# Attention of layer 0: value products of two groups in one PSUM tile, with one copy, turn and division per pair

## The reference, cut to what matters

```python
qvk = (h @ Wqvk).reshape(b, s, 3, H, HD)
q, v, k = (qvk[:, :, 0], qvk[:, :, 1], qvk[:, :, 2])
scores = jnp.einsum('bshi,bthi->bsth', q, k)
...
scores = scores + mask[None, :, :, None]
scores = scores / math.sqrt(d)
weights = jax.nn.softmax(scores, axis=2)
wv = jnp.einsum('bsth,bthi->bshi', weights, v).reshape(b, s, d)
return wv @ Wo
```

## Time and profile before

| what | value |
|---|---|
| median of 3 runs | 783.85 us (783.3 to 787.15) |
| span of the profiled execution | 765.3 us |
| median of the runs less that span | 18.55 us |
| PE busy | 703.9 us, 92% |
| PEld (weight loads) busy | 526.3 us, 69% |
| DVE busy | 546.6 us, 71% |
| ACT busy | 419.5 us, 55% |
| POOL busy | 327.7 us, 43% |
| mean granted TensorE clock | 0.994 of full speed |

### The profile page before, as it was taken

How to read it: one execution, slowest core, us unless ns; L and a number is a source line. 1 busy time by engine, 2 the same in 40 slices (tenths; PEclk the granted TensorE clock), 3 DMA queues, 4 the chain that set the end, 5 groups by cost and what they waited for, 6 DMA issues and landing times.

```text
span 765.3 us, 17690 instructions
## 1 busy us (share of the span) xinstructions
PE 703.9 (92%) x6133; PEld 526.3 (69%) x6133; DVE 546.6 (71%) x1053; ACT 419.5 (55%) x802; POOL 327.7 (43%) x433
## 2 busy tenths in 40 slices
PE   5787788998899978989898999999999999999997
PEld 4643445556755547757666888888888888888885
DVE  6878997885678866779886766666665666666665
ACT  5645665676477678677664444444444444444442
POOL 3765643783758860147694631212122221222222
PEclk9999999999999999999999999999999999999999
DMA  6984655431134420012114611112121212111100
GB/s 188 261 239 137 179 133 201 167 95 49 51 120 129 142 85 1 12 33 61 54 43 117 156 52 56 56 41 69 41 69 41 69 41 59 50 52 58 41 15 14
DMA packets 63795, 66.51 MB, mean 87 GB/s; under 512 B 6512, under 2 KB 41840, under 8 KB 63728
## 3 DMA queue, kind: packets, MB, share of 16 engines
q1 hardware_dynamic: 62128, 63.23, 27.7%
q0 software_dynamic: 1024, 2.12, 1.0%
q10 hardware_dynamic: 576, 0.27, 0.1%
HBM read 47.46 MB, written 17.99 MB: 86 GB/s over the span
## 4 chain that ended last, share of the span: by engine, by line
PE 75%; DVE 9%; issue 5%; ACT 4%; DMA 3%; POOL 2%; SPq 1%; ACTq 0%; POOLq 0%; DVEq 0%
PE ps L1763 25%; PE ps L1992 22%; PE ps L1876 3%; DVE m L1241 3%; PE ps L1683 3%; PE ps L1587 3%; PE ps L1796 2%; PE ps L1831 2%; PE ps L1593 2%; PE ps L1597 2%; PE ps L1897 1%; DMA qk_parts<-qk_p 1%; PE ps L1601 1%; PE ps L1688 1%; PE ps L1580 1%
## 5 line engine op out<-in xcount | busy, mean ns | idle before, releaser
L963 ACT ACTIVATE f_h<-ps 128x512 fp32r<-128x512 f32 x256 | 153.3, 599 | 197.6 <-PE ps L1763 197.6
L1463 DVE SCALAR_TENSOR_TENSOR f_l<-ps,f_h 128x512 fp32r<-128x512 f32 x256 | 175.9, 691 | 112.5 <-ACT f_h L963 111.3
L1763 PE MATMUL ps<-x_hl,w_h 128*128 (+1 forms) x512 | 200.3, 391 | 0.0
L783 POOL TENSOR_TENSOR acc<-acc,yt 128x512 f32<-128x512 f32 x55 | 70.9, 1289 | 249.8 <-DVE yt L1501 249.8
L877 ACT ACTIVATE probs<-ps 128x1536 f32<-128x1536 f32 x64 | 92.8, 1450 | 34.4 <-PE ps L1606 33.8
L1763 PEld LDWEIGHTS ps<-x_hl,w_h 128*128 128x128 f32 x512 | 96.1, 188 | 19.6
L682 POOL TENSOR_SCALAR_AFFINE_SELECT probs<-probs 128x512 f32<-128x512 f32 x128 | 78.4, 637 | 59.8 <-ACT probs L877 59.5
L1992 PE MATMUL ps<-f_l,w_h 128*128 128x512 f32 x256 | 99.8, 390 | 1.3 <-DVE f_l L1463 1.3
L1992 PE MATMUL ps<-f_h,w_h 128*128 128x512 f32 x256 | 99.7, 390 | 0.0
L1763 PE MATMUL ps<-x_hl,w_l 128*128 (+1 forms) x256 | 99.6, 389 | 0.0
L1992 PE MATMUL ps<-f_h,w_l 128*128 128x512 f32 x256 | 99.6, 389 | 0.0
(11 more groups left out here) (225 smaller groups left out, 1328.2 us busy)
## 6 DMA issues: line engine op xcount, KB each, us to landing
gate_b<-gate_rows SPq DMA_DIRECT2D x64, 256.0 KB, 3.3
qk_parts<-qk_p SPq DMA_DIRECT2D x16, 512.0 KB, 3.8
k_st<-qk_parts SPq DMA_DIRECT2D x64, 96.0 KB
q_st<-qk_parts SPq DMA_DIRECT2D x64, 96.0 KB
y_tok<-zero SPq DMA_DIRECT2D x8, 512.0 KB, 2.9
w_raw<-in_w_e SPq DMA_DIRECT2D x16, 256.0 KB, 2.7
x_rows<-xn_rows SPq DMA_DIRECT2D x8, 260.0 KB, 3.2
w_up<-in_w_up SPq DMA_DIRECT2D x8, 256.0 KB, 2.7
```

Of the source, the lines that this page charges most:

```text
L783: nc.gpsimd.tensor_tensor(acc[:, :], acc[:, :], yt[:, e % 2, :], ALU.add).then_inc(summed, 1)
L963: nc.scalar.activation(r32(f_h[:, m % 4, :]), ps[:, m % 4, :], ACT.Relu).then_inc(f_hi, 1)
L1463: nc.vector.scalar_tensor_tensor(out=r32(f_l[:, m % 4, :]), in0=ps[:, m % 4, :], scalar=0.0, in1=f_h[:, m % 4, :], op0=ALU.max, op1=ALU.su ...
L1763: last = nc.tensor.matmul(dst, r32(lhs[i]), r32(rhs[j]), start=(k == 0), stop=(k == 2))
```

## The change

- `v_ring` has 48 columns per pair of heads in place of 16 per head: values of the first head, ones, zeros, then values of the second and ones. An even group multiplies with columns 0 to 31 and starts the accumulation; the odd group multiplies with columns 16 to 47 and ends it. Each product gives 32 rows.
- The copy from PSUM (`evacuate_pair`), the turning (`turn_out`) and the division (`divide_pair`) happen once per pair: copy in even slots, turning and division in odd slots. The turning stands ahead of `mask_late`, and so does the search for the experts' slots (slot 21).
- Both tiles of turned heads are made in one slot.
- `ps_m` lies in bank 0, in the bank of the early scores. So `mask_early` of the next group waits for `mneg_done` instead of `early_max`, and it stands inside `scores`, behind L1597 and the first two of the four L1601. `weigh` no longer waits for `mneg_done`.
- At the start, the maxima of group 1 are turned before the scores of group 2.
- The host permutes the weights of queries and keys so that pairs of heads fit (`by_depth`).

```diff
-        v_ring = sb("v_ring", [P, 2, TB, H0, 2 * HD0], where=era)
+        v_ring = sb("v_ring", [P, 2, TB, H0 // 2, 6 * HD0], where=era)
...
-            return 4 * b + 8 + (t if b < B - 2 else 0)
+            return 4 * b + 8
...
-        ps_m = ps[0:2 * GH, 6, S:S + P]
+        ps_m = ps[0:2 * GH, 0, 0:P]
...
-            nc.gpsimd.memset(v_ring[:, :, :, :, :], 1.0).then_inc(zeroed, 1)
+            nc.gpsimd.memset(v_ring[:, :, :, :, :], 0.0).then_inc(zeroed, 1)
             pool.wait_ge(zeroed, 6)
+            nc.gpsimd.memset(v_ring.rearrange("p u t i c -> p (u t i) c")[:, :, HD0:5 * HD0 + 1:4 * HD0], 1.0).then_inc(zeroed, 1)
+            pool.wait_ge(zeroed, 7)
...
-            def evacuate(g):
-                act.wait_ge(pv_done, num(g) + 1)
-                if past(g, 2):
-                    act.wait_ge(o_turned, num(g) - 1)
-                nc.scalar.activation(o_ring[:, at(g, 2), :], ps_o, ACT.Copy).then_inc(o_evac, 1)
+            def evacuate_pair(i):
+                act.wait_ge(pv_done, 2 * i + 2)
+                if i >= 2:
+                    act.wait_ge(o_turned, i - 1)
+                nc.scalar.activation(o_ring[:, i % 2, :], ps_o, ACT.Copy).then_inc(o_evac, 1)
...
-                if past(g, 3) and within(plus(g, -3), G0):
-                    evacuate(plus(g, -3))
+                if num(g) % 2 == 0 and 4 <= num(g) <= G0 + 2:
+                    evacuate_pair(num(g) // 2 - 2)
...
                     act.wait_ge(rstd_ready, B + 2)
+                    act.wait_ge(pv_done, G0 - 1)
...
-                if n >= 4 and within(plus(g, -4), G0):
-                    divide(plus(g, -4))
+                if n % 2 == 1 and 5 <= n <= G0 + 3:
+                    divide_pair((n - 5) // 2)
...
+                nc.vector.reciprocal(rden[:, i % 2, :, :], heads[:, :, :, HD0]).then_inc(inverted, 1)
+                dve.wait_ge(inverted, i + 1)
+                nc.vector.tensor_tensor(wv_tok[:, b % 2, :, half * D // 2:(half + 1) * D // 2].rearrange("p t (h d) -> p t h d", h=2 * GH),
+                                        heads[:, :, :, 0:HD0], rden[:, i % 2, :, :].unsqueeze(3).broadcast_to([P, TB, 2 * GH, HD0]), ALU.mult).then_inc(wv_put, 1)
...
                 if past(g, 2):
-                    pe.wait_ge(early_max, before_it(g))
+                    pe.wait_ge(mneg_done, num(g))
...
                 pe.wait_ge(mrow_in[at(g, 4)], div(g, 4) * 16 + 16)
+                for u in range(2):
+                    turned_first(g, u, 0)
+                if both:
+                    mask_early(far)
                 for n in range(2):
...
-                for n in range(2):
-                    for u in range(2):
-                        turned_first(g, u, n)
+                for u in range(2):
+                    turned_first(g, u, 1)
...
-                if past(g, 1):
-                    pe.wait_ge(o_evac, num(g))
-                pe.wait_ge(mneg_done, min(n + 3, G0))
-                if n >= 8 and n % GPB0 < TB:
-                    pe.wait_ge(wvn_done, (n - 8) // GPB0 * TB + (n % GPB0 + 1 if n < G0 else TB))
+                if num(g) % 2 == 0 and num(g) >= 2:
+                    pe.wait_ge(o_evac, num(g) // 2)
+                if n >= 8 and n % GPB0 == 0:
+                    pe.wait_ge(wvn_done, (n - 8) // GPB0 * TB + TB)
+                rows = slice(k % 2 * 2 * HD0, k % 2 * 2 * HD0 + 4 * HD0)
                 for h in range(GH):
-                    nc.tensor.matmul(ps_o[32 * h:32 * h + 2 * HD0, :], v_ring[:, u, 0, k * GH + h, :],
+                    nc.tensor.matmul(ps_o[32 * h:32 * h + 4 * HD0, :], v_ring[:, u, 0, k // 2 * GH + h, rows],
...
-                                     start=True, stop=False, skip_group_check=True)
+                                     start=(k % 2 == 0), stop=False, skip_group_check=True)
...
+                if n == 2:
+                    turn_max((0, 1))
+                    keep_on(7, 2)
                 scores_alone((0, n))
-                if n:
+                if n == 1:
                     keep_on(7, 2)
-                    turn_max((0, n - 1))
+                    turn_max((0, 0))
                     keep_on(7, 2)
...
+                if n == FIND:
+                    pe.wait_ge(wv_put, (FIND - 5) // 2)
+                    find_slots()
+                if n % 2 == 1 and 5 <= n <= G0 + 3:
+                    turn_out((n - 5) // 2)
                 if within(plus(g, 3), G0):
                     mask_late(plus(g, 3))
...
-                if past(g, 4) and within(plus(g, -4), G0):
-                    turn_out(plus(g, -4))
                 if within(plus(g, 2), G0):
                     turn_max(plus(g, 2))
-                if within(plus(g, 3), G0):
-                    mask_early(plus(g, 3))
...
-            def turn_out(g):
-                pe.wait_ge(o_evac, num(g) + 1)
-                if past(g, 1):
-                    pe.wait_ge(wv_put, num(g))
-                if g[1] % GPB0 == 3 and past(g, 7):
-                    pe.wait_ge(x_attn, div(plus(g, -7), GPB0) + 1)
+            def turn_out(i):
+                pe.wait_ge(o_evac, i + 1)
+                if i >= 1:
+                    pe.wait_ge(wv_put, i)
+                if i % 2 == 1 and i >= 3:
+                    pe.wait_ge(x_attn, (i - 3) // 2 + 1)
```

More of the change, by code:

```diff
@@ L155, in build @@
         wvn = sb("wvn", [P, 2, S], where=era)
-        rden = sb("rden", [P, 2, TB, GH], where=era)
-        v_ring = sb("v_ring", [P, 2, TB, H0, 2 * HD0], where=era)
+        rden = sb("rden", [P, 2, TB, 2 * GH], where=era)
+        v_ring = sb("v_ring", [P, 2, TB, H0 // 2, 6 * HD0], where=era)
         m8 = sb("m8", [P, 2, GH, TB], where=era)
@@ L855, in put_heads0 @@
             def put_heads0(b, t):
-                act.wait_ge(wv_mm, 2 * b + t + 1 if b < B - 2 else 2 * b + 2)
+                act.wait_ge(wv_mm, 2 * b + 2)
                 if b >= 2:
                     act.wait_ge(wo_mm, b - 1)
-                nc.scalar.activation(wvn[:, b % 2, t * P:(t + 1) * P], ps_heads(t if b >= B - 2 else 0), ACT.Copy).then_inc(wvn_done, 1)
+                nc.scalar.activation(wvn[:, b % 2, t * P:(t + 1) * P], ps_heads(t), ACT.Copy).then_inc(wvn_done, 1)
             for n in range(2):
@@ L866, in slot @@
                     negate_max(plus(g, 2))
-                if past(g, 3) and within(plus(g, -3), G0):
-                    evacuate(plus(g, -3))
+                if num(g) % 2 == 0 and 4 <= num(g) <= G0 + 2:
+                    evacuate_pair(num(g) // 2 - 2)
                 for b in range(B):
-                    for t in range(TB):
-                        if heads_turned(b, t) == num(g):
+                    if heads_turned(b) == num(g):
+                        for t in range(TB):
                             put_heads0(b, t)
@@ L1317, in low_x, with divide_pair @@
                 nc.vector.tensor_tensor(r32(x_hl[:, 1, ds(b * S, S)]), ps_t1(v % 2), x_hl[:, 0, ds(b * S, S)], ALU.subtract).then_inc(xl_put, 1)
[L1319 to L1329, removed]
+            def divide_pair(i):
+                b, half = divmod(i, 2)
+                dve.wait_ge(o_turned, i + 1)
+                if half == 0 and b >= 2:
+                    dve.wait_ge(wv_mm, 2 * b - 2)
+                heads = ps_tok.rearrange("p (t h r) -> p t h r", t=TB, h=2 * GH)
+                nc.vector.reciprocal(rden[:, i % 2, :, :], heads[:, :, :, HD0]).then_inc(inverted, 1)
+                dve.wait_ge(inverted, i + 1)
+                nc.vector.tensor_tensor(wv_tok[:, b % 2, :, half * D // 2:(half + 1) * D // 2].rearrange("p t (h d) -> p t h d", h=2 * GH),
+                                        heads[:, :, :, 0:HD0], rden[:, i % 2, :, :].unsqueeze(3).broadcast_to([P, TB, 2 * GH, HD0]), ALU.mult).then_inc(wv_put, 1)
             def add_attention(b):
@@ L1724, in slot @@
                         attention_out(b)
-                    for t in range(TB):
-                        if heads_turned(b, t) == n:
-                            turn_heads(b, t)
+                    if heads_turned(b) == n:
+                        turn_heads(b)
                 if n == COUNT:
                     pe.wait_ge(counted, 3)
-                if n == FIND:
-                    pe.wait_ge(wv_put, FIND - 4)
-                    find_slots()
-                if past(g, 4) and within(plus(g, -4), G0):
-                    turn_out(plus(g, -4))
                 if within(plus(g, 2), G0):
                     turn_max(plus(g, 2))
-                if within(plus(g, 3), G0):
-                    mask_early(plus(g, 3))
                 if within(g, G0):
```

29 lines of the change are left out of this document (15 added, 14 removed).

## The result

The changed kernel takes 789.3 us (median of 9 runs, 787.32 to 792.29) against 786.2 for the kernel before on the same chip (9 runs): ratio 1.006, 95% interval 1.0046 to 1.0075. It is slower by 0.6%; the forecast was 781.6, range 775.0 to 786.5. A second comparison, with the set of runs 1 to 4, gives the same, 1.0064 (1.0039 to 1.0088).

The account below looks back on a forecast made before the run. DVE's loop (2.77 us) bound most slots, PE's path (3.03) those with attention output, DVE's routing work eleven slots. Terms 1.0 - 0.4 - 4.3 + 2.6 - 1.1 = -2.2 took 783.85 to 781.6 us, range 775 to 786.5.

Parts of the forecast that it names:

- start-up: First slots: group 1's maxima must leave the bank before group 2's scores, 1.7 late, 0.7 given back: +1.0, bounds 0.5 and 1.7.
- slots 0 to 8 and 20 to 23: Forecast for slots 3 to 8 and 21 to 23: routing work on DVE, divisions gone from even slots; estimate -0.4 us.
- 8 to 20: DVE-bound routing stage, eleven slots: 34.0 against 38.35 us, -4.3.
- steady, 37 slots: 15 slots before the experts and 22 after go from 2.85 to 2.92 us on PE's path: +2.6.
- end: Last groups: one round of copy, turn and division leaves the final chain: -1.1 us, bounds 0 and -2.5.
- all under PE's 2.86 and 3.09, which take over: Routing stage: plain DVE slots of 2.8, 2.3 and 2.7 us fall below PE's path, which then sets them.
- ACT's loop with a late negation, 2.75: On ACT, when negated maxima come behind the exponential, the loop becomes 2.75 us, below PE's.
- The idle 0.55 before the division goes too: Routing stage on DVE: the 0.55 us wait for turned outputs vanishes, since they are turned half a slot earlier.
- The two crossings more, 0.20 a slot: On PE, the moved mask adds two changes between all-row and half-row matmuls, 0.10 us each: +0.20.
- The second rival: Mask's wait for negated maxima becomes the bound; at 0.2 latency 0.13 late in 53 slots, +6.9, 788.5 us; chance 0.15.
- the prediction's own sign (above 0.05 a slot): The forecast would be wrong if PE's wait for the negated maxima were above 0.05 us a slot.
- 18.5 us lie outside the span: Profiled execution spans 765.3 us, median 783.85; the 18.5 more was put around the span and left alone.

Follow-up runs that it names:

- runs 1 to 4: Kernel before again, 784.35 us; changed kernel again, 789.69; kernel before with only moved maxima and mask, 789.9; with only pairing, sums lost, 777.27.
- runs 1, 2: The kernel before, unchanged, for a second profile: 784.35 us; the changed kernel, unchanged, for a second profile: 789.69 us.
- run 3: Kernel before with only the maxima moved to the early scores' bank, the early mask moved and the changed start order: 789.9 us, ratio 1.008.
- run 1: The kernel before, unchanged, for a second profile: 784.35 us, ratio 0.9998, span 779.1.
- Run 7: Changed kernel with one more 32-column matmul over 48 rows in each of the 64 slots: ratio 1.0079 to the kernel before.
- Run 8: Changed kernel with ACT's four token-mark scalings moved from behind the exponential to ahead of the next one: ratio 1.0062 to the kernel before.
- runs 6, 7: Changed kernel with one more 32-column matmul per slot, over 128 rows: ratio 1.0169 to before; over 48 rows: 1.0079.
- run 5: Kernel before with pairing alone, sums kept by plain fp32 matmuls without start flag for odd maxima and second heads' turn: 768.16 us, ratio 0.9962.
- run 9: Kernel before with pairing alone, sums kept by turns without start flag for odd maxima and second heads' turn: 774.24 us, ratio 0.9874.

## Why the prediction was wrong

In the order of its own sum:

| term | forecast | measured | from |
|---|---|---|---|
| start-up | +1.0 | +1.3 | POOL's L619/L621 to the first exponential, 4.12 and 5.45 |
| slots 0 to 8 and 20 to 23 (forecast: 3 to 8, 21 to 23) | -0.4 | +2.2 | runs 1, 2 |
| 8 to 20 | -4.3 | -2.8 | runs 1, 2 |
| steady, 37 slots | +2.6 | +4.1 | rounds 11.41 and 11.85 |
| end | -1.1 | -0.8 at full clock, -0.1 to -0.2 in its own profiles | below |
| sum | -2.2 | +4.0 to +4.7 | ratio: +5.0 |

**No single step turned the sign. Three terms came out worse by 1.5 to 2.6 us each, the start by 0.3 and the end by up to 1.0.** The mechanisms in the steady slots were right and sizes off.

The sum is a little short of what was measured. In the set of runs 1 to 4 the median span grows from 781.9 to 788.0, 6.1 us, since 0.9 of what lay outside the span is gone. The 1.4 to 2.1 us that no term has are in part clock, for which the forecast had no term at all: the median granted clock goes from 0.984 to 0.980, and slot 40 alone loses some 1.8. Whether the change brings this on stays open.

*Slots 0 to 8,* the largest miss. I had put slots 3 to 8 and 21 to 23 at an estimate of -0.4 without a slot-by-slot sum, and for slots 0 to 2 I had no term; they take 0.9 more. PE's path, 2.9 to 3.0, binds slots 0, 4 and 5, which were 2.77 to 2.80. In slot 6 (3.62 against 3.03) the division is gone from DVE, but what comes next on DVE waits 0.91 for ACT's exponential of the routing weights, which stands behind the big one. I had not asked what was late next. Another 0.9 is clock, as far as run 7 tells: a stretch at 1.2 GHz of 6.8 us in both profiles of the changed kernel and in run 3, 3.4 in run 1. Run 7, with the same order and 3.4 us of it, takes 28.8 instead of 29.7.

*8 to 20.* "all under PE's 2.86 and 3.09, which take over" failed in slots 9 to 12. The eleven slots that the forecast put at 34.0 take 35.7. I had worked out ACT's loop with a late negation, 2.75, and left out that ACT marks tokens for 0.61 in just these four slots; with it my own figure is 3.36. Run 8 shows it. It accounts for 0.9 of the 1.7 us. Besides, "The idle 0.55 before the division goes too" is wrong: 0.45 is left, since the turn now follows the value products, which end no earlier than DVE's maxima.

*Steady.* Slots of 2.93, 2.88 and 3.11 where I had 2.86, 2.86 and 3.09. In the slot of 2.93 shown above two terms were too small: the two turns, now right behind the value products, take 0.27 to L1590 instead of 0.22, and the products of 32 rows 0.45 from L1689 to L1694, not 0.43 (I had bounded them by 0 and 0.05 and taken 0). The half groups, 0.47 and 0.22 for 0.45 and 0.24, cancel. The two crossings more, 0.20 a slot, were right (runs 6, 7), and they are what makes this part a loss: 7.4 us over 37 slots, against 4.1 in all.

*End.* In run 8 the last pair of turns of values starts 11.9 us after the exponential of group 61, before 12.7 (in both profiles): 0.8 gained. In both profiles of the changed kernel itself, where a half-clock stretch starts 8 us after that exponential, it is 12.4 and 12.5, so most of the gain is gone. From group 61 to the end these two profiles take 1.9 and 3.5 us more than run 1, with one half-clock stretch of 3.4 us more; that time lies behind the part that was changed.

*The second rival* (the new wait becomes the bound from a latency of 0.1) is refuted as I had put it: negation to mask is 0.05 to 0.06. Where ACT has other work between, or in the stalls, the wait is real: in the profile of the changed kernel PE idles 5.6 us before this mask in nine slots, 1.4 of it in slots 9 to 12 and 4.2 in the stalls. By the prediction's own sign (above 0.05 a slot) that was too much.

*The profile read.* Stating that 18.5 us lie outside the span was wrong; 2.6 do. It left the sum alone, but some 16 us, stalls and half clock among them, were thereby out of sight, and with them the terms for which I had no row.

Right: DVE's loop no longer binds the steady slots (9 to 6% of the chain); L1675 to L1600 0.21 for 0.42; 32 copies on ACT. The rounds of either part alone, worked out from the same terms but after the result, came to 0.04 us.

## What to carry to other kernels

Two changes that touch different engines must be summed slot by slot as a maximum over loops, not as a sum of gains: here -6 and +6 made +5, and though the steady slots added up, the slots of other stages did not. Read a second profile, and compare its span with the runs, before a difference between the two is called time outside the span. Count the crossings between full-row and half-row matmuls when an instruction is moved; here, at 0.10 each, two of them cost PE as much as the 0.21 that the move took off DVE's loop. And where an in-order engine now feeds a wait, list all it does between, stage by stage, not in the steady slot alone.

## Not expected of the hardware

- The same kernel takes 784 us on two chips and 771 on a third. POOL's sixteen gathers take 0.97 each on all three, but on the first two PE stalls for 0.3 to 1.6 us in about half of the slots in which they run, and on the third next to never. Why is open, and was not tried.
- In run 5 a plain fp32 matmul of 8 columns of weights against an identity stands as two instructions and takes 0.31; a turn of the same data once, 0.11.
- An fp32 turn without the start flag overwrites where the bank's marks are clear and leaves the pending sums of other columns alone (run 9).
- Nine filler matmuls more in a gap of PE went with a half-clock stretch less in one kernel and with a longer one in another (one profile each).
